# Turning the row maxima of a diffusion transformer's attention with VectorE and DRAM in place of TensorE

## The chip, the cores and the metric

The kernel runs on one core of one Trainium2 chip. The metric is the device time of one execution in microseconds (us); lower is better.

## The reference, cut to what matters

Sixteen images of 256 tokens by 256 features pass through four layers. Layers 0, 2 and 3 are full ones: self attention, cross attention to 120 context tokens, and an MLP of width 1024. Layer 1 has cross attention alone. There are 16 heads of 16 features, all in float32. Of it the change touches only the softmax of the two attentions:

```python
attn = jnp.einsum('bhnd,bhsd->bhns', q, k) * SCALE
attn = jax.nn.softmax(attn, axis=-1)
o = jnp.einsum('bhns,bhsd->bhnd', attn, v)
```

For every query and head the softmax subtracts the largest score of the row before the exponential.

## The kernel before, in words

**Two passes over the scores.** An attention (F is self attention, G cross attention) of one image first makes its scores with the queries in the partitions: steps S0 to S3 for F, S0 and S1 for G (L1287). After each, VectorE takes the maxima over the keys (L978) into `row_max`, 128 queries by 16 heads for each half of the 256 tokens. Then the scores are made again with the keys in the partitions: T0 to T3 for F, T0 and T1 for G (L1309). A last matmul of each T step adds minus the maximum of each query (L1314): it multiplies a one-hot selector `sel` with `max_t`, which must have the heads in the partitions and the 256 queries along the free axis. ScalarE takes the exponential (L1117), and the PV steps (L1340) multiply by the values into `o_acc`; VectorE divides and turns the result in O0 and O1 (L1000 to L1011).

**How the maxima get turned.** Step X (L979 to L992, VectorE) writes minus the maximum in two parts, high and low, for every head into `max_parts`: 128 columns for each half of the tokens, most of them zero. Step M then turns them: TensorE transposes the two 128x128 blocks into a PSUM bank (L1291 to L1295, by way of the helper on L1144), and ScalarE copies the bank to `max_t` (L1103 to L1107). T0 waits for that copy (L1302). There are 48 F jobs and 64 G jobs, so 112 of these turns.

**One score buffer, three ring banks.** S and T steps all use the one four-bank PSUM tensor `score`. TensorE may start the next S or T step only when VectorE's maxima (after an S) or ScalarE's exponential (after a T) have read the one before (L1178 to L1181 and L1193 to L1196). All other matmuls (projections Q, K, V, KV, PR, the MLP's H0 to H3 and F20, F21, the transposes LN and C, and M) go to `ring`, three PSUM banks taken in turn (`RING_STEPS`, L156); a bank is taken again when its reader is done. `o_acc` is one bank, too.

**The order is written out by hand.** Every engine walks the same list of steps and does its own part of each. A word such as `G.T0` names a part (P, F, A for self attention; R, G, B for cross attention; E for the MLP; a leading 1 for layer 1) and a step; `AHEAD` (L145) says which image a part works on in a turn. A word that ends in `.d` marks where VectorE, GpSimd and SyncE do their share of a step, later than TensorE and ScalarE. The first three turns are the list START (L84), the turns 3 to 21 are WITH_L1 (L64), which have layer 1's cross attention in them as well, the turns 22 to 46 are TURN (L49), and the end is TAIL (L116). Since each S or T step has to wait for the reader of the last one, the words on one line of these lists are the work that stands between two score steps.

**SyncE's queue** issues all transfers in the order of the list: q and k are laid out for the scores after the steps Q, K and KV (L646 to L663; four and six transfers), the gates are loaded (`gld`, L716), images are loaded and stored. A wait on SyncE holds up all that stands behind it. `gate_rows` (L284) is a DRAM tensor that the kernel writes and reads again.

Of the kernel before, what the change touches and what calls it, by code (L numbers as in the profile page):

```python
# [13 lines left out]
P = 128  # L14
# [33 lines left out]

TURN = """  # L49
F.S0 f.O1 f.PV3 E.H0  # L50
F.S1 P.V E.RES E.H1 P.V.d
F.S2 P.LN E.H2
F.S3 E.H3 p.N P.gld A.PR F.X A.PR.d
G.S0 F.M B.PR B.PR.d R.C
G.S1 E.F20a E.F20b G.X
F.T0 E.F20b.d R.N P.Q e.N G.M R.A
F.T1 e.A p.A P.Q.d P.K F.PV0
G.T0 c.NC P.RES F.PV1 P.K.d
P.ld R.LN e.LN F.O0 R.RES G.O0
G.T1 E.gld c.AC P.ST R.KV R.KV.d E.F21a G.O1 G.PV0  # L60
F.T2 R.Q G.PV1
F.T3 E.F21b E.F21b.d F.PV2 R.Q.d c.ld
""".split()
# [1336 lines left out]
```

## Time and profile before

| | us |
|---|---|
| median of three runs | 2577.09 |
| lowest, highest | 2574.03, 2577.36 |
| the profiled execution | 2577.71 |
| its span in the profile | 2575.9 |
| TensorE (PE) busy in it | 2479.3 |
| VectorE (DVE) busy | 1858.5 |
| ScalarE (ACT) busy | 1274.0 |
| GpSimd (POOL) busy | 467.2 |

The span is the profiled execution without the 1.8 us around it. Busy time is the union of the instructions of an engine, and ends of matmuls are modelled, so short gaps between matmuls can be hidden in it.

### The profile page before, as it was taken

The page shows a single profiled execution, that of the slowest core. Times are in us where ns is not written, and L with a number is a line of the kernel's source. Part 1 is how long each engine was busy: PE and PEld are TensorE (multiplying, and loading weights), DVE is VectorE, ACT ScalarE, POOL GpSimd, SP SyncE. Part 2 cuts the span into 40 slices and gives each one's busy share as a digit, 9 for nine tenths or more (in the row PEclk, how much of TensorE's full clock was granted, in tenths as well). Part 3 has the DMA queues.
Part 4 walks back from the last instruction along what each step waited for, and adds up shares of the span by engine and source line. Part 5 has one row for each costly group of instructions (what it writes and reads, how often), then busy time and mean ns, then how long its engine had stood idle before and what let it go on. Part 6 is the DMA issues. An engine that isn't in the chain of part 4 may idle for free.

```text
span 2575.9 us, 66165 instructions
## 1 busy us (share of the span) xinstructions
PE 2479.3 (96%) x27466; PEld 1848.3 (72%) x27466; DVE 1858.5 (72%) x3532; ACT 1274.0 (49%) x1810; POOL 467.2 (18%) x510
## 2 busy tenths in 40 slices
PE   5779999999999999999999999999999999999998
PEld 3557777777777777777777777777777777777767
DVE  4767777777777777777777767777677677776752
ACT  1345544555555555555455554554555545445443
POOL 0111211212111211111121211211212212112121
PEclk7889999999999999999999999999999999999999
DMA  5322222222222223232122122132231222222211
GB/s 188 129 93 78 78 74 74 74 80 87 83 77 76 90 81 96 77 101 68 56 76 74 56 76 74 62 96 78 80 107 60 82 84 78 78 66 80 82 33 42
DMA packets 236749, 207.56 MB, mean 81 GB/s; under 512 B 87682, under 2 KB 222020, under 8 KB 236452
## 3 DMA queue, kind: packets, MB, share of 16 engines
q1 hardware_dynamic: 236452, 203.32, 24.7%
q8 instruction: 220, 3.60, 0.6%
q14 instruction: 77, 0.63, 0.1%
HBM read 58.34 MB, written 4.39 MB: 24 GB/s over the span
## 4 chain that ended last, share of the span: by engine, by line
PE 79%; DVE 12%; issue 3%; ACT 3%; SPq 2%; DMA 1%; POOL 1%; DVEq 0%; POOLq 0%; ACTq 0%
PE o_acc L1340 11%; PE score L1287 10%; PE ring L1371 10%; PE ring L1248 10%; PE ring L1362 10%; PE score L1309 8%; PE ring L1352 6%; DVE row_max_F L978 5%; DVE row_max_G L978 5%; PE ring L1144 4%; PE ring L1256 3%; PE score L1314 3%; PE ring L1268 2%; ACT probs L1117 2%; PE ring L1271 2%
## 5 line engine op out<-in xcount | busy, mean ns | idle before, releaser
L1117 ACT ACTIVATE probs<-score 120x2048 f32<-120x2048 f32 (+1 forms) x320 | 601.6, 1880 | 374.8 <-PE score L1314 368.0
L978 DVE TENSOR_REDUCE row_max_F<-score 128x8 f32<-128x2048 f32 x192 | 438.7, 2285 | 103.3 <-PE score L1287 102.8
L1371 PE MATMUL ring<-w_fc,h_t 128*128 128x256 f32 x1536 | 368.9, 386 | 1.0 <-ACT h_t L1128 1.0
L1362 PE MATMUL ring<-x_t_E,w_fc 128*128 128x256 f32 x1536 | 368.3, 386 | 0.0
L978 DVE TENSOR_REDUCE row_max_G<-score 128x16 f32<-128x1920 f32 x128 | 276.1, 2157 | 116.8 <-PE score L1287 116.8
L1128 ACT ACTIVATE h_t<-ring,cols 128x256 f32<-128x256 f32 x384 | 160.7, 470 | 341.1 <-PE ring L1362 341.0
L1362 PEld LDWEIGHTS ring<-x_t_E,w_fc 128*128 128x128 f32 x1536 | 280.8, 190 | 59.3 <-issue 20.3
L1000 DVE STREAM_TRANSPOSE o_turned<-o_acc 128x512 f32<-128x512 f32 x224 | 159.9, 714 | 220.3 <-PE o_acc L1340 220.3
L1371 PEld LDWEIGHTS ring<-w_fc,h_t 128*128 128x128 f32 x1536 | 282.5, 190 | 46.3 <-ACT h_t L1128 1.4
L1340 PE MATMUL o_acc<-probs,v_self 128*17 128x256 f32 x3072 | 204.3, 384 | 0.0
L793 POOL TENSOR_TENSOR x<-x,gated 128x256 f32<-128x256 f32 x96 | 70.3, 733 | 723.1 <-DVE gated L1032 723.1
L1248 PE MATMUL ring<-x_t_P,w_qk 128*128 128x256 f32 x768 | 197.8, 403 | 1.2 <-ACT x_t_P L1068 1.2
L1309 PE MATMUL score<-q_F,k_F 32*128 32x256 f32 x3072 | 166.6, 303 | 8.9 <-ACT probs L1117 5.7
L1309 PEld LDWEIGHTS score<-q_F,k_F 32*128 32x128 f32 x3072 | 119.3, 184 | 75.2 <-issue 55.7
L1248 PEld LDWEIGHTS ring<-x_t_P,w_qk 128*128 128x128 f32 x768 | 143.9, 197 | 35.2 <-issue 8.4
L1287 PEld LDWEIGHTS score<-k_F,q_F 32*128 32x128 f32 x3072 | 106.4, 188 | 84.2 <-DVE row_max_F L978 42.0
L1287 PE MATMUL score<-k_F,q_F 32*128 32x256 f32 x3072 | 146.3, 307 | 21.4 <-DVE row_max_F L978 18.5
L1287 PEld LDWEIGHTS score<-k_G,q_G 32*128 32x128 f32 x4096 | 125.3, 187 | 52.4 <-DVE row_max_G L978 28.0
L1287 PE MATMUL score<-k_G,q_G 32*128 32x120 f32 x4096 | 142.9, 277 | 14.8 <-DVE row_max_G L978 12.0
L787 POOL TENSOR_TENSOR x<-x,gated 128x512 f32<-128x512 f32 x48 | 60.8, 1267 | 423.0 <-DVE gated L1019 423.0
L1340 PE MATMUL o_acc<-probs,v_ctx 120*17 120x256 f32 x2048 | 135.5, 382 | 0.0
L1099 ACT ACTIVATE q_parts<-ring,cols 128x256 fp32r<-128x256 f32 x224 | 94.0, 472 | 80.9 <-PE ring L1248 78.9
(136 smaller groups left out, 3770.9 us busy)
## 6 DMA issues: line engine op xcount, KB each, us to landing
q_G<-q_parts SPq DMA_DIRECT2D x256, 128.0 KB, 2.1
q_F<-q_parts SPq DMA_DIRECT2D x192, 128.0 KB, 2.1
k_F<-k_parts SPq DMA_DIRECT2D x96, 256.0 KB, 2.5
k_F<-k_parts SPq DMA_DIRECT2D x192, 128.0 KB, 2.2
k_G<-k_parts SPq DMA_DIRECT2D x128, 120.0 KB, 2.2
k_G<-k_parts SPq DMA_DIRECT2D x256, 60.0 KB, 1.9
gate_now_P<-gate_rows SPq DMA_DIRECT2D x48, 256.0 KB, 3.2
gate_now_E<-gate_rows SPq DMA_DIRECT2D x48, 256.0 KB, 3.4
```

The source lines that it names most:

```text
L978: nc.vector.tensor_reduce(dst, src, AX.X, ALU.max).then_inc(row_max_ready[r].sem, 1)
L1000: nc.vector.transpose(o_turned[:, :, :, :].rearrange("p i b d -> p (i b d)"), o_acc[:, :])\
L1117: nc.scalar.activation(probs[v % 2][0:keys, :, :], score[0:keys, :].rearrange("p (h q) -> p h q", h=2 * GROUPS), ACT.Exp, scale=SCALE).the ...
L1128: last = nc.scalar.activation(h_t[:, c, :], ps[:, c % 2 * NT:(c % 2 + 1) * NT], ACT.Gelu_apprx_tanh, bias=col(m, "fc1", c))
L1144: return nc.tensor.transpose(dst, src, ident[0:rows_in, 0:rows_in])
L1248: last = mm(ps[:, c * NT:(c + 1) * NT], weight[:, k, at + c * P:at + (c + 1) * P], buffer(x_t, r, m, n)[:, k, :], start=k == 0, stop=k == ...
L1287: last = mm(score[:, col0:col0 + width], q_now[at, c, e, tile * P:(tile + 1) * P].bitcast(F32R), k_now[at, two, c, e, :].bitcast(F32R), st ...
L1309: mm(score[0:keys, g * BANK + e * NT:g * BANK + (e + 1) * NT], k_now[at, two, c, e, tile * P:tile * P + keys].bitcast(F32R), q_now[at, c, ...
L1340: last = mm(o_acc[32 * j:32 * j + HD + 1, i * NT:(i + 1) * NT], v_head, probs[v % 2][0:keys, 2 * j + i, :], start=tile == 0 and (i == 0 or ...
L1352: last = mm(ps[:, t * D:(t + 1) * D], buffer(o_t, r, m, n)[:, k, t * P:(t + 1) * P], weight[:, k, :], start=k == 0, stop=k == KC - 1)
L1362: last = mm(ps[:, c % 2 * NT:(c % 2 + 1) * NT], w_fc1[:, k, c * P:(c + 1) * P], buffer(x_t, r, m, n)[:, k, :], start=k == 0, stop=k == KC - 1)
L1371: last = mm(ps[:, 0:D], h_t[:, k, t * P:(t + 1) * P], w_fc2[:, k, :], start=k == 0, stop=k == MC - 1)
```

## The change

Step M no longer uses TensorE, ScalarE or a ring bank. `max_parts` shrinks to 64 columns (two halves of 32: 16 heads times two parts). VectorE turns it in 32x32 squares at the end of step X. At X SyncE stores the turned squares in a DRAM tensor `max_rows` of 32 rows by 256 queries, which puts the squares side by side. At M SyncE waits for that transfer and loads the 32 rows into `max_t` four times, once for each group of 32 partitions. T0 on TensorE waits for the load. `sel` picks other rows accordingly, and two memsets go. The lists TURN, WITH_L1 and START have a new order throughout, TAIL has the word E14.gld at another place.

```diff
@@ -46,72 +46,73 @@
 
 
 
+
 TURN = """
-F.S0 f.O1 f.PV3 E.H0
-F.S1 P.V E.RES E.H1 P.V.d
-F.S2 P.LN E.H2
-F.S3 E.H3 p.N P.gld A.PR F.X A.PR.d
-G.S0 F.M B.PR B.PR.d R.C
-G.S1 E.F20a E.F20b G.X
-F.T0 E.F20b.d R.N P.Q e.N G.M R.A
-F.T1 e.A p.A P.Q.d P.K F.PV0
-G.T0 c.NC P.RES F.PV1 P.K.d
-P.ld R.LN e.LN F.O0 R.RES G.O0
-G.T1 E.gld c.AC P.ST R.KV R.KV.d E.F21a G.O1 G.PV0
-F.T2 R.Q G.PV1
-F.T3 E.F21b E.F21b.d F.PV2 R.Q.d c.ld
+F.S0 f.PV3 f.O1 E.H0
+F.S1 E.RES P.V E.H1 P.V.d
+F.S2 p.N E.H2 P.LN
+F.S3 E.H3 A.PR F.X A.PR.d
+G.S0 F.M R.C B.PR
+G.S1 B.PR.d E.F20a E.F20b
+F.T0 e.N G.X R.N e.A G.M P.Q R.A P.Q.d
+F.T1
+P.ld F.PV0 E.F20b.d P.K
+G.T0 R.RES c.NC P.K.d F.O0 R.LN e.LN G.O0 F.PV1
+G.T1 R.KV G.PV0 E.F21a E.gld
+F.T2 R.KV.d R.Q G.PV1
+F.T3 G.O1 E.F21b c.AC c.ld p.A P.gld P.RES F.PV2 R.Q.d E.F21b.d P.ST
 """.split()
 WITH_L1 = """
-F.S0 f.PV3 E.H0
-F.S1 1R.C P.V P.V.d P.LN
-F.S2 P.gld E.H1 f.O1 E.H2
-F.S3 F.X 1R.LN E.RES E.H3
-1G.S0 A.PR F.M A.PR.d
-1G.S1 1G.X B.PR E.F20a
-G.S0 E.F20b 1G.M B.PR.d
+F.S0 E.RES 1R.RES f.PV3 E.H0
+F.S1 P.LN P.V P.V.d
+F.S2 E.H1 E.H2 f.O1
+F.S3 1R.LN E.H3
+1G.S0 A.PR B.PR A.PR.d
+1G.S1 P.gld B.PR.d 1R.C E.F20a 1G.X 1G.M
+G.S0 E.F20b F.X R.C E.F20b.d
 G.S1 E.F21a
-1G.T0 1R.RES E.F20b.d P.Q e.N
-1G.T1 R.N e.A P.Q.d 1G.PV0 R.RES G.X 1G.O0 P.K
+1G.T0 e.N P.Q F.M R.N G.X
+1G.T1 P.Q.d 1G.PV0 P.K
 F.T0 E.F21b 1G.PV1
-F.T1 G.M F.PV0 P.K.d R.A
-P.ld 1R.Q E.F21b.d
-G.T0 F.PV1 1G.O1 R.C p.N p.A 1R.KV 1R.Q.d F.O0
-G.T1 G.PV0 1R.KV.d G.O0 R.LN 1B.PR 1p.N 1p.NC
-F.T2 G.PV1 G.O1 R.Q E.gld R.Q.d P.RES
-F.T3 R.KV P.ST 1p.AC 1R.ld 1B.PR.d F.PV2 c.ld 1p.A R.KV.d e.LN
+F.T1 G.M 1p.NC R.A 1R.Q P.K.d 1G.O0 1R.ld E.F21b.d 1G.O1 F.PV0
+G.T0 F.PV1 R.LN 1R.KV e.A 1p.N p.N F.O0 1R.Q.d
+G.T1 R.RES G.PV0 1R.KV.d G.O0 e.LN 1B.PR
+P.ld E.gld 1B.PR.d
+F.T2 P.RES G.O1 G.PV1 R.Q p.A P.ST
+F.T3 R.Q.d 1p.A R.KV R.KV.d c.ld 1p.AC F.PV2
 """.split()
 
 START = """
-W0.v Z0.ZT Z0.ZC P0.N P0.ld P0.A Z0.ZM Z0.ZX W0.cpb W0.proj Z0.ZL P0.LN Z0.ZA W0.raw Z1.ZL P2.ld W0.fc1 P0.Q
-P1.ld W0.self P0.Q.d Z1.ZA P0.K Z0.ZS0 P0.K.d Z1.ZC Z2.ZL Z2.ZA W0.cross P1.N Z0.ZG Z1.ZM Z1.ZX
-F0.S0 P1.A
-F0.S1 P0.V P0.V.d
-F0.S2 P1.LN Z0.ZS1 Z2.ZC
-F0.S3 Z2.ZG Z3.ZL Z2.ZS1 F0.X Z2.ZM Z2.ZX F0.M
-F0.T0 P2.N Z3.ZC R0.ld P1.Q Z3.ZA P1.Q.d F0.PV0
-F0.T1 P1.K Z2.ZS0
-F0.T2 P1.K.d Z3.ZM F0.PV1 P1.V
-F0.T3 P3.ld F0.PV2 F0.O0 Z3.ZG
-F1.S0 W0.fc2 R0.C P1.V.d
-F1.S1 P5.ld P2.A F0.PV3 W0.v2
-F1.S2 F0.O1
-F1.S3 P2.LN P0.RES P0.gld F1.X A0.PR A0.PR.d F1.M
-F1.T0 R0.N Z3.ZX R0.RES P2.Q P2.Q.d R1.ld
-F1.T1 P2.K R0.A P3.N R0.LN P2.K.d F1.PV0 P2.V F1.PV1
-F1.T2 Z3.ZS1 R0.Q P2.V.d
-F1.T3 F1.O0 R0.KV P3.A
-F2.S0 P1.RES W1.l1 F1.PV2 R2.ld R0.KV.d W0.cp
-F2.S1 R0.Q.d
-F2.S2 F1.PV3 F1.O1
-F2.S3 A1.PR F2.X P4.ld
-G0.S0 F2.M
+P0.ld W0.raw P0.N P0.A Z0.ZT Z0.ZC Z0.ZM Z0.ZX Z0.ZL Z0.ZA W0.proj P1.ld Z1.ZL W0.fc1 W0.self P0.LN Z1.ZA P0.Q
+P1.N P0.Q.d Z0.ZG P0.K P0.K.d W0.v Z0.ZS0 Z2.ZA W0.cpb Z2.ZL Z0.ZS1 Z1.ZM Z1.ZC Z1.ZX P1.A
+F0.S0 P0.V P0.V.d P2.ld
+F0.S1
+F0.S2 P1.LN Z2.ZC Z3.ZL W0.cross
+F0.S3 Z2.ZG F0.X F0.M Z2.ZM Z2.ZX P2.N Z3.ZA Z3.ZC
+F0.T0 P1.Q P1.K P1.Q.d P1.K.d F0.PV0 P0.RES Z2.ZS0
+F0.T1
+F0.T2 R0.ld F0.O0 W0.fc2 P0.gld P3.ld F0.PV1 Z3.ZM
+F0.T3 P1.V
+F1.S0 R0.C P2.A F0.PV2 Z2.ZS1 F0.PV3
+F1.S1 F0.O1
+F1.S2 P1.V.d
+F1.S3 F1.X W0.v2 P3.N Z3.ZG P2.LN A0.PR A0.PR.d Z3.ZX P2.Q R0.N F1.M
+F1.T0 R0.A P2.Q.d
+F1.T1 P1.RES R0.RES P2.K
+F1.T2 F1.PV0 P2.V R0.LN R1.ld
+F1.T3 W0.cp P5.ld F1.PV1 P2.K.d P2.V.d R0.Q F1.PV2 F1.O0
+F2.S0 R0.KV R0.KV.d R1.C
+F2.S1 Z3.ZS1 R0.Q.d
+F2.S2 F1.PV3 P4.ld F1.O1
+F2.S3 P1.gld F2.X A1.PR
+G0.S0 F2.M P3.A
 G0.S1 A1.PR.d P3.LN
-F2.T0 G0.X P1.gld R1.C P3.Q G0.M
-F2.T1 P3.K
-G0.T0 R1.N P3.Q.d P3.K.d R1.A F2.PV0 R1.LN F2.PV1 P4.N
-G0.T1 F2.O0 R1.Q G0.O0 G0.PV0
-F2.T2 Z3.ZS0 R1.Q.d G0.O1 P2.RES G0.PV1
-F2.T3 P4.A R1.KV R1.KV.d R1.RES R3.ld P2.gld F2.PV2
+F2.T0 P3.Q G0.X
+F2.T1 G0.M P3.K
+G0.T0 W1.l1 F2.PV0 P4.N P3.Q.d R1.N R1.A P3.K.d P2.gld R1.LN F2.PV1 F2.O0
+G0.T1 G0.O0 R1.Q R2.ld G0.PV0
+F2.T2 G0.PV1 P2.RES P4.A R1.KV R1.Q.d G0.O1
+F2.T3 R1.KV.d R3.ld R1.RES F2.PV2 Z3.ZS0
 """.split()
 TAIL = """
 P15.gld
@@ -134,12 +135,12 @@
 G14.T1 G14.O1 G14.PV0 R15.KV E12.F21a G14.PV1 E13.H0 R15.KV.d E12.F21b E12.F21b.d E13.RES E13.H1 E13.H2
 E13.gld E13.H3
 G15.S0 B14.PR B14.PR.d E14.N
-G15.S1 E13.F20a E13.F20b E14.gld G15.X G15.M
+G15.S1 E13.F20a E13.F20b G15.X G15.M
 G15.T0 E14.LN E14.A
 G15.T1 P12.ST E13.F20b.d G15.PV0 E13.F21a G15.O0 E13.F21b G15.O1 G15.PV1 E14.H0 E14.H2 E14.H1 E14.H3
-E13.F21b.d B15.PR E15.gld E14.F20a B15.PR.d E15.N P13.ST E14.F21a E15.LN E14.F20b E14.RES E15.A E14.F21b
-E15.RES E15.H0 P15.ST E15.H1 E15.H2 E15.H3 E15.F20a E14.F20b.d E15.F21a E15.F20b P14.ST E15.F21b E14.F21b.d
-E15.F20b.d E15.F21b.d
+E13.F21b.d E14.gld B15.PR E15.gld E14.F20a B15.PR.d E15.N P13.ST E14.F21a E15.LN E14.F20b E14.RES E15.A
+E14.F21b E15.RES E15.H0 P15.ST E15.H1 E15.H2 E15.H3 E15.F20a E14.F20b.d E15.F21a E15.F20b P14.ST E15.F21b
+E14.F21b.d E15.F20b.d E15.F21b.d
 """.split()
 
...
-RING_STEPS = ("LN", "C", "Q", "K", "V", "KV", "M", "PR", "H0", "H1", "H2", "H3", "F20a", "F21a",
+RING_STEPS = ("LN", "C", "Q", "K", "V", "KV", "PR", "H0", "H1", "H2", "H3", "F20a", "F21a",
               "ZT", "ZC", "ZM", "ZX", "ZG")
...
+        max_rows = {r: nc.dram_tensor(f"max_rows_{r}", [32, NT], F32, kind="Internal").ap() for r in "FG"}
...
-        max_parts = {r: sb(f"max_parts_{r}", [P, TT, P]) for r in "FG"}
+        max_parts = {r: sb(f"max_parts_{r}", [P, TT, GROUPS, PAIRS, 2]) for r in "FG"}
+        max_turned = {r: sb(f"max_turned_{r}", [P, TT, 32]) for r in "FG"}
...
+                if step == "X":
+                    sp.wait_ge(max_turned_ready[r].sem, max_turned_ready[r].after(m, n))
+                    if max_laid[r].order[m, n] > 0:
+                        sp.wait_ge(max_laid[r].sem(m, n), max_laid[r].after(m, n) - 16)
+
+                    sp.dma_start(max_rows[r].rearrange("h (t a q) -> a h t q", t=TT, a=4), max_turned[r][:, :, :])\
+                        .then_inc(max_written[r].sem(m, n), 16)
+                elif step == "M":
+                    sp.wait_ge(max_written[r].sem(m, n), max_written[r].after(m, n))
+                    t_psum[r].wait_before(sp, m, n)
+                    sp.dma_start(max_t[r][:, :], max_rows[r].unsqueeze(0).to_broadcast([GROUPS, 32, NT]))\
+                        .then_inc(max_laid[r].sem(m, n), 16)
...
-            for r in "FG":
-                nc.gpsimd.memset(max_parts[r][:, :, :], 0.0).then_inc(const_ready, 1)
...
-            nc.vector.tensor_reduce(pair_rows[:, :], ident[:, :].rearrange("p (g w) -> p g w", g=GROUPS)[:, :, 0:8]
-                                    .rearrange("p g (c e) -> p c g e", e=2), AX.XY, ALU.add)\
-                .then_inc(pair_rows_ready, 1)
+            for g in range(GROUPS):
+                at = slice(32 * g, 32 * (g + 1))
+                last = nc.vector.tensor_reduce(pair_rows[at, :], ident[at, 40 * g:40 * g + 2 * PAIRS]
+                                               .rearrange("p (c e) -> p c e", e=2), AX.X, ALU.add)
+            last.then_inc(pair_rows_ready, 1)
...
                     src = row_max[r][:, :, :, :].rearrange("p t g c -> p (t g) c")
-                    parts = max_parts[r][:, :, :].rearrange("p t (g w) -> p (t g) w", g=GROUPS)[:, :, 0:2 * PAIRS]\
-                        .rearrange("p b (c e) -> p b c e", e=2)
-                    if m == 0 and n == 0:
-                        dve.wait_ge(const_ready, CONSTS)
-                    m_psum[r].wait_before(dve, m, n)
+                    parts = max_parts[r][:, :, :, :, :].rearrange("p t g c e -> p (t g) c e")
+                    max_turned_ready[r].wait_before(dve, m, n)
                     dve.wait_ge(row_max_ready[r].sem, row_max_ready[r].after(m, n))
                     nc.vector.tensor_scalar(parts[:, :, :, 0].bitcast(F32R), src, -1.0, None, ALU.mult)\
                         .then_inc(max_hi_ready[r].sem, 1)
@@ -990,6 +1003,12 @@
                     nc.vector.scalar_tensor_tensor(out=parts[:, :, :, 1].bitcast(F32R), in0=src, scalar=-1.0,
                                                    in1=parts[:, :, :, 0], op0=ALU.mult, op1=ALU.subtract)\
                         .then_inc(max_parts_ready[r].sem, 1)
+                    dve.wait_ge(max_parts_ready[r].sem, max_parts_ready[r].after(m, n))
+                    if max_written[r].order[m, n] > 0:
+                        dve.wait_ge(max_written[r].sem(m, n), max_written[r].after(m, n) - 16)
+                    nc.vector.transpose(max_turned[r][:, :, :].rearrange("p t h -> p (t h)"),
+                                        max_parts[r][:, :, :, :, :].rearrange("p t g c e -> p (t g c e)"))\
+                        .then_inc(max_turned_ready[r].sem, 1)
...
-                elif step == "M":
-                    act.wait_ge(m_psum[r].sem, m_psum[r].after(m, n))
-                    t_psum[r].wait_before(act, m, n)
-                    nc.scalar.activation(max_t[r][:, :].bitcast(F32R), ps[:, 0:NT], ACT.Identity)\
-                        .then_inc(max_t_ready[r].sem, 1)
...
-                elif step == "M":
-                    pe.wait_ge(max_t_ready[r].sem, max_t_ready[r].after(m, n))
...
-                elif step == "M":
-                    pe.wait_ge(max_parts_ready[r].sem, max_parts_ready[r].after(m, n))
-                    for t in range(TT):
-                        last = transpose(ps[:, t * P:(t + 1) * P], max_parts[r][:, t, :], P)
-                    last.then_inc(m_psum[r].sem, 1)
...
-                        pe.wait_ge(max_t_ready[r].sem, max_t_ready[r].after(m, n))
+                        pe.wait_ge(max_laid[r].sem(m, n), max_laid[r].after(m, n))
```

The rest of the diff declares or drops the semaphores that these lines use (`max_turned_ready`, `max_written` and `max_laid` come, `m_psum` and `max_t_ready` go).

## Rows read from the trace of the kernel before

**Rows 1.** the page: busy shares of the engines, and the chain that ended last, by engine

```profile
...
PE 2479.3 (96%) x27466; PEld 1848.3 (72%) x27466; DVE 1858.5 (72%) x3532; ACT 1274.0 (49%) x1810; POOL 467.2 (18%) x510
...
PE 79%; DVE 12%; issue 3%; ACT 3%; SPq 2%; DMA 1%; POOL 1%; DVEq 0%; POOLq 0%; ACTq 0%
...
```

**Rows 2.** busy us by stage: PE, PEld, DVE, ACT, POOL; then PEclk, DMA share, GB/s

```profile
...
0.00:150.80 150.80, 104.67 (x1086) 71.21 (x1086) 88.26 (x184) 44.82 (x58) 12.74 (x26) 0.83 0.45 150
...
300.00:1265.60 965.60, 949.54 (x11015) 703.79 (x11014) 743.70 (x1424) 501.33 (x712) 174.87 (x187) 1.00 0.25 80
1265.60:2432.20 1166.60, 1161.78 (x12751) 873.27 (x12750) 849.27 (x1587) 601.63 (x853) 223.28 (x238) 1.00 0.24 76
2432.20:2575.90 143.70, 128.95 (x1128) 100.19 (x1124) 68.49 (x128) 58.27 (x91) 25.07 (x28) 0.98 0.14 45
...
```

**Rows 3.** groups by line and shape: count | busy us, mean ns | idle before

```profile
...
L978 DVE TENSOR_REDUCE row_max_F<-score 128x8 f32<-128x2048 f32 x192 | 438.7, 2285 | 103.3 <-PE score L1287 102.8
...
L1000 DVE STREAM_TRANSPOSE o_turned<-o_acc 128x512 f32<-128x512 f32 x224 | 159.9, 714 | 220.3 <-PE o_acc L1340 220.3
...
L1011 DVE STREAM_TRANSPOSE o_t_B<-o_norm 128x256 f32<-128x256 f32 x128 | 57.0, 445 | 4.4
...
L1144 PE MATMUL ring<-ident,max_parts_G 128*128 128x128 f32 x128 | 25.6, 281 | 0.0
...
L1144 PE MATMUL ring<-ident,max_parts_F 128*128 128x128 f32 x96 | 20.3, 294 | 0.8 <-DVE max_parts_F L990 0.8
...
```

**Rows 4.** TensorE in one turn with layer 1: start us, us

```profile
...
740.33 0.38 PE L1144 MATMUL ring<-ident,max_parts_F 128*128 128x128 f32 x2
740.90 1.11 PE L1287 MATMUL score<-k_G,q_G 32*128 32x120 f32 x32 [0.19 <-DVE row_max_G L978]
...
743.77 1.89 PE L1371 MATMUL ring<-w_fc,h_t 128*128 128x256 f32 x8
745.59 1.11 PE L1287 MATMUL score<-k_G,q_G 32*128 32x120 f32 x32
...
749.04 1.11 PE L1287 MATMUL score<-k_G,q_G 32*128 32x120 f32 x32 [0.20 <-DVE row_max_G L978]
...
752.41 0.50 PE L1309 MATMUL score<-q_G,k_G 32*120 32x256 f32 x8 [0.34 <-DVE row_max_G L978]
...
```

**Rows 5.** TensorE in one turn without layer 1: start us, us

```profile
...
2029.42 0.44 PE L1144 MATMUL ring<-ident,max_parts_F 128*128 128x128 f32 x2
2029.69 1.89 PE L1352 MATMUL ring<-w_cp,o_t_B 128*128 128x256 f32 x8
2031.42 0.37 PE L1144 MATMUL ring<-ident,x_hat_C 120*128 120x120 f32 x2
2031.82 1.11 PE L1287 MATMUL score<-k_G,q_G 32*128 32x120 f32 x32
...
2039.25 0.38 PE L1144 MATMUL ring<-ident,max_parts_G 128*128 128x128 f32 x2
2039.56 0.51 PE L1309 MATMUL score<-q_F,k_F 32*128 32x256 f32 x8
...
```

**Rows 6.** DMA issues: KB each, us to landing

```profile
...
gate_now_E<-gate_rows SPq DMA_DIRECT2D x48, 256.0 KB, 3.4
...
context<-in_ctx_dram SPq DMA_DIRECT2D x32, 120.0 KB, 2.3
...
gate_rows<-h_t SPq DMA_DIRECT2D x6, 32.0 KB, 2.1
...
```

**Rows 7.** all engines near the end: VectorE's X, then TensorE's T0

```profile
...
2495.67 0.19 DVE L990 SCALAR_TENSOR_TENSOR max_parts_G<-row_max_G,max_parts_G 128x32 fp32r<-128x32 f32 x1
...
2496.98 0.51 PE L1309 MATMUL score<-q_G,k_G 32*120 32x256 f32 x8 [0.57 <-ACT max_t_G L1106]
...
```

**Rows 8.** TensorE in turn 3: start us, us

```profile
...
160.82 1.23 PE L1287 MATMUL score<-k_F,q_F 32*128 32x256 f32 x16 [2.87 <-DVE row_max_F L978]
162.76 3.75 PE L1352 MATMUL ring<-w_proj,o_t_A 128*128 128x256 f32 x8 [0.71 <-DVE o_t_A L1011]
...
```

More of the change, by code:

```diff
@@ L382, in build_program @@
         s_psum = signals("s_psum", "FG", {"F": 4, "G": 2})
-        m_psum = signals("m_psum", "FG")
         t_psum = signals("t_psum", "FG", {"F": 4, "G": 2})
@@ L394, in build_program @@
         k_high_ready = signals("k_high_ready", "FG")
-        max_t_ready = signals("max_t_ready", "FG")
         probs_ready = signals("probs_ready", "FG", {"F": 4, "G": 2})
@@ L409, in build_program @@
         max_parts_ready = signals("max_parts_ready", "FG")
+        max_turned_ready = signals("max_turned_ready", "FG")
         o_turned_ready = signals("o_turned_ready", "FG", 2)
@@ L429, in build_program @@
         k_laid = semaphore("k_laid")
+        max_written = {r: Turns([semaphore(f"max_written_{r}")], self_order if r == "F" else cross_order) for r in "FG"}
+        max_laid = {r: Turns([semaphore(f"max_laid_{r}")], self_order if r == "F" else cross_order) for r in "FG"}
         x_stored = semaphore("x_stored")
@@ L473, in build_program @@
         projects = {"F": "A", "G": "B"}
-        CONSTS = 8
+        CONSTS = 6
         q_jobs = [(attends[r], m, n) for r, m, step, n, here in steps if step == "Q"]
```

## The prediction

> **What bounds the kernel now.** I read the page's busy shares and its chain first: TensorE is busy 96% of the span and holds 79% of the chain, VectorE holds 12% [rows 1]. Then the stages. The turns 6 to 21 (with layer 1) take 965.6 us, 60.4 each; the turns 22 to 46 take 1166.6, 46.7 each. TensorE stands idle for only 16 us of the first and 5 us of the second; head and tail lose 46 and 15 us [rows 2]. By these shares any work taken from TensorE should come off the time. The timeline of single turns says otherwise, and that decides my forecast: `score` is one buffer, so between two S or T steps there is a least distance. After a G S step of 1.04 us the next score step begins 3.4 us after the start of the last (745.59 to 749.04, and 749.04 to 752.41), each time with an idle of 0.2 to 0.3 us released by VectorE's maxima [rows 4]; the maxima themselves take 2.29 us for F [rows 3] and a little less for G. Where the ring work in such a slot is shorter than about 2.4 us, it is free, and taking it away gives a wait.
>
> **What step M costs.** TensorE is busy 25.6 + 20.3 = 45.9 us with the 224 transposes [rows 3], 0.41 us for each of 112 jobs; from start to start a pair takes 0.27 or 0.31 us [rows 5], about 33 us in all. Those are the upper ends of what can be won.
>
> Where do they stand? **Turns with layer 1** have three. The ones after 1G.S0 and before G.S1 stand in slots that VectorE ends: M at 740.33 is over at 740.6, and the next S starts at 740.90 on the maxima [rows 4]. They win nothing where they are. In the new list their places are taken: 1G.S0's slot gets both PR steps (3.65 us, no wait), 1G.S1's and G.S0's slots get a C transpose beside F20a or F20b : 0.27 to 0.40 [rows 5] and 1.82 from 743.77 to 745.59 [rows 4] are 2.1 to 2.2, again under 2.4. The three slots were 3.44 + 4.69 + 3.45 = 11.58 us and become 4.69 + 3.44 + 3.44, and 0.15 more, since VectorE does B.PR.d and X with its new turn before G.S0's maxima: 11.72, so +0.14. The two C steps left other slots: -0.53, but F.S1's slot then holds only LN and V (2.4) and waits 0.12. F.T1's slot loses an M and is long enough (1R.Q and a PV remain, 2.9): -0.36. Sum -0.63, say -0.6 for each turn, **-10 us** for 16 turns.
>
> **Turns without layer 1.** G.S0's slot holds M, PR and C: 0.27 + 1.73 + 0.40 = 2.40, exactly the least distance [rows 5]. The new list keeps C and PR there: 2.13 of work and 0.27 of wait, nothing won. F.T0's slot holds Q and M, 2039.56 being the next T; the exponential would let T1 start 0.1 earlier, and without M it does. The other slots keep their work. -0.1 for each turn, **-2.5 us** for 25. So some 14 us of M's time in these turns becomes wait.
>
> **What is added on VectorE.** A transpose of 64 columns. The two in the trace take 714 ns for 512 and 445 for 256 columns [rows 3], 1.05 ns a column, hence 0.24 us; ends are 0.19 (the smallest operation beside it [rows 7]) and 0.445. 112 x 0.24 = 27 us on an engine busy 72% [rows 1]; its only exposed part is the 0.15 above. The four small reductions that make `sel`, the two memsets less and the 112 ScalarE copies less all lie beside longer waits: nothing.
>
> **What is added as latency.** The store: 32 KB to DRAM; the nearest row lands in 2.1 us, the other end is the 3.4 of a 256 KB broadcast from DRAM. The load: 128 KB in 1 KB rows; the nearest is the context load, 120 KB in the same shape, 2.3 us, and I add 0.2 for reading each row four times; the same 3.4 is its upper end and 2.1 the lower for both [rows 6]. With SyncE's own 0.1 that is 4.8 us from the end of X's turn to T0 (4.3 to 6.9). On SyncE's queue the M of an image waits about 2 us for its store; behind it stand P.Q's and P.K's layouts, which have most of a turn until the next F.S0, so I give nothing for that. P.gld now stands ahead of 1G.X, but what it waits for is done in the slot before.
>
> Is the latency covered? The tightest places: 1G.X ends 4.7 us after the start of 1G.S1 (step 1.15, maxima 2.2, B.PR.d 0.68, X 0.7), 1G.T0 is due at 10.3 (three S slots): 5.6 us against 4.8. G.X in a turn without layer 1 ends 4.85 after G.S1's end, G.T0 is due at 10.4: 5.6 against 4.8. Both are covered with 0.8 to spare; the F jobs have over 3 us.
>
> Here the Trainium skill speaks against the change: DMA: Bandwidth & Descriptors, Specifications, says that transfers with pieces below 512 B are written by read-modify-write, and the store consists of 128-byte pieces. No row here shows such a store to DRAM; it enters the sum with nothing, and its sign is that of the second rival.
>
> **The tail** keeps its order but for a gate load, and there nothing covers the latency. In G14, X ends at 2495.86 and T0 starts at 2496.98 [rows 7]; now it would be 2495.9 + 0.25 + 4.8 = 2500.9, 3.9 later. G15 has the same pattern, 3.9 again. Some 2 us of the first are taken up by waits for x_hat that follow it anyway; F15.M's own place saves 1; I add 2 for a lower granted clock after these gaps (the head, full of gaps, has a mean of 0.83 against 1.00 in the turns [rows 2]). **+7 us**.
>
> **The head.** TensorE idles for 46 of 150.8 us [rows 2]. The new list asks for x, w_raw and the conditioning vector earlier and lets P0.K's layout no longer wait behind Z0's gates and loads: some 3.5 us earlier F0.S0. Against this F0.M's and F1.M's latency is exposed (about +3 and +1), and denser T slots give 2 or 3 back: -2. In turn 3 PR waits 0.71 for o_t after an S step that had itself waited 2.87, and then runs at half pace, 3.75 against 1.89 for the same step in rows 5 [rows 8]; the new list moves O1 a slot forward and puts both PR steps behind S3: -4 with the filled slot before. Turns 4 and 5: -1. **-7 us**, and this is the least certain term (-17 to +6).
>
> **Sum.** -10 - 2.5 + 7 - 7 = -12.5. The profiled execution took 2577.71 (span 2575.9 and 1.8 around it), 0.6 above the median of 2577.09. From the median: 2564.6, rounded 2565.
>
> **The rivals.**
> First, all of TensorE's M time comes off: for it speaks the 99.6% busy share in the turns 22 to 46, against it the slots of rows 4 and 5. It gives 2577 - 46 + 7 = 2538, or 2551 with the 33 us of pitch. Chance 0.13.
> Second, the way through DRAM lands late, at 1G.T0 and G.T0 of each turn. With both transfers at 3.4 us the latency is 6.9, 2.1 more than I take; 0.8 is spare, so 1.3 us is lost in 16 + 25 turns, 53 us: 2618. It decides from 1.1 us above my value (0.8 and 12.5/41 = 0.3): 5.9 us. Against it: the 2.1 and 2.3 of rows 6 are medians under the same traffic. With the excess halfway it is 2590. Chance 0.14. The skill's rule on small pieces would bring this one about.
> Third, the orders win nothing: head and tail cost more than I think (gaps lower the clock), and the turns' -12 is used up: 2577, within 0.2%. Chance 0.13.
> My forecast: 0.60, with its own range 2552 to 2572.
>
> **Range and chances.** 2546 to 2588 takes in most of the first rival by pitch, the third, and the mild part of the second. A measurement of this kernel can tell about 0.2%, 5 us, from no change. Faster by more: 0.60 + 0.13 = 0.73, less 0.02 for the top of my own range, 0.71. Within it: 0.14. Slower: 0.15.
>
> **What would show it.** Right: M's transposes and the copies are gone; the turns with layer 1 last about 59.8 us and those without 46.6; TensorE's busy time falls by some 40 us and its idle time rises by some 30, with "VectorE's maxima" as releaser of the score steps. 1G.T0 and G.T0 start on the exponential or the maxima, not on the load of `max_t`; in G14 and G15 T0 does wait for that load, 4 us. The store lands in about 2.1 us, the load in 2.5; VectorE's turn is 0.24. Wrong: T0 waiting for the load in every turn (second rival), or TensorE's idle time unchanged (first), or F3.S0 later than 150.9 us.

## The result, and the profile after

| | before | after |
|---|---|---|
| median of four runs each, us | 2575.56 | 2649.62 |
| lowest, highest | 2573.84, 2577.36 | 2640.79, 2653.45 |
| span of the profiled execution | 2575.9 | 2647.8 |

The ratio is 1.0283 (95% interval 1.0255 to 1.031): the change makes the kernel 74 us slower. I had forecast 2565, and the range ended at 2588.

The first lines to read are the page's busy shares and its chain, which answer to [rows 1]:

```profile
PE 2473.2 (93%) x27242; PEld 1827.6 (69%) x27242; DVE 1850.2 (70%) x3647; ACT 1236.5 (47%) x1698; POOL 467.1 (18%) x508
...
PE 66%; DVE 13%; DMA 12%; issue 6%; ACT 2%; SPq 1%; POOL 0%; DVEq 0%; POOLq 0%; ACTq 0%
```

The 224 transposes and 112 copies are gone. TensorE's busy time falls by only 6 us, though, where I had 40. DMA held 1% of the chain and now holds 12%, TensorE's share falls from 79% to 66%. The waits of TensorE (us in total, times, longest) say on what:

```profile
PE score L1316 <- DMA max_t_G<-max_rows_G: 72.5, 47, 6.8
...
PE score L1316 <- DMA max_t_F<-max_rows_F: 4.6, 4, 1.9
```

T0 of cross attention waits for the load of `max_t` 47 times. Which of its two transfers is late? The timeline of one turn without layer 1, all engines, start and us:

```profile
2083.57 0.24 DVE L1009 STREAM_TRANSPOSE max_turned_G<-max_parts_G 128x64 f32<-128x64 f32 x1
...
2083.84 0.52 SPq L681 DMA_DIRECT2D max_rows_G<-max_turned_G  x1
...
2086.17 0.52 SPq L686 DMA_DIRECT2D max_t_G<-max_rows_G  x1
...
2091.26 0.51 PE L1316 MATMUL score<-q_G,k_G 32*120 32x256 f32 x8 [1.70 <-DMA max_t_G<-max_rows_G]
```

VectorE's turn takes the 0.24 us of the forecast. SyncE waits for the store before it issues the load, so the store has landed 2.33 us after its issue. The load then takes 5.09 us until T0 starts, where I had 2.5. In a turn with layer 1, TensorE:

```profile
775.08 0.50 PE L1316 MATMUL score<-q_G,k_G 32*120 32x256 f32 x8 [1.87 <-DMA max_t_G<-max_rows_G]
...
775.98 3.41 PE L1260 MATMUL ring<-x_t_P,w_qk 128*128 128x256 f32 x8
```

The load was issued at 770.57, 4.51 us before. Behind the wait the projection Q takes 3.41 us, where [rows 5] have 1.89 for a step of as many matmuls; the clock granted in these 3.41 us is 0.56 of full, and in T0 just ahead of them still 1.00. The tail shows it most, TensorE again:

```profile
2559.96 0.79 PE L1316 MATMUL score<-q_G,k_G 32*120 32x256 f32 x8 [6.58 <-DMA max_t_G<-max_rows_G]
...
2564.22 3.75 PE L1260 MATMUL ring<-x_t_R,w_q 128*128 128x256 f32 x8 [0.72 <-ACT x_t_R L1087]
```

There the granted clock is 0.50, the lower of the two levels (1.2 for 2.4 GHz). But the kernel before had short waits at this place too, and its Q already took 3.15 us:

```profile
2501.15 3.15 PE L1248 MATMUL ring<-x_t_R,w_q 128*128 128x256 f32 x8
```

By stage, the columns as in [rows 2]; the bounds are the starts of F.S0 in turns 3, 6, 22 and 47:

```profile
0.00:163.10 163.10, 108.73 (x1082) 71.91 (x1082) 88.80 (x193) 43.49 (x54) 14.70 (x26) 0.80 0.45 143
163.10:318.20 155.10, 135.38 (x1484) 99.98 (x1484) 106.20 (x216) 67.79 (x94) 27.05 (x29) 0.94 0.28 86
318.20:1294.40 976.20, 936.65 (x10926) 692.74 (x10922) 744.25 (x1472) 485.07 (x665) 179.93 (x188) 1.00 0.29 87
1294.40:2490.10 1195.70, 1159.80 (x12658) 860.27 (x12654) 841.92 (x1639) 583.50 (x801) 218.81 (x236) 1.00 0.26 81
2490.10:2647.80 157.70, 132.66 (x1116) 102.73 (x1116) 69.04 (x131) 56.68 (x87) 26.66 (x29) 0.93 0.16 47
```

All stages are longer: 12.3 us to turn 3, 5.9 in turns 3 to 5, 10.6 in turns 6 to 21, 29.1 in turns 22 to 46 and 14.0 in the tail, whose granted clock is 0.93 for 0.98 before.

### The profile page after: what moved, and what is told of

It reads as the page before. It is cut to its first block, busy times and chain, and to the rows that moved or that the text cites. A ratio compares the mean times of both kernels' runs of the same rounds, so it can differ in the third digit from the quotient of the medians.

```text
span 2647.8 us, 66048 instructions
## 1 busy us (share of the span) xinstructions
PE 2473.2 (93%) x27242; PEld 1827.6 (69%) x27242; DVE 1850.2 (70%) x3647; ACT 1236.5 (47%) x1698; POOL 467.1 (18%) x508
## 4 chain that ended last, share of the span: by engine, by line
PE 66%; DVE 13%; DMA 12%; issue 6%; ACT 2%; SPq 1%; POOL 0%; DVEq 0%; POOLq 0%; ACTq 0%
PE ring L1369 11%; PE o_acc L1347 10%; PE score L1299 9%; DMA max_t_G<-max_rows_G 8%; PE score L1316 7%; PE ring L1260 7%; PE ring L1359 6%; PE ring L1378 5%; DVE row_max_F L994 5%; DMA max_rows_G<-max_turned_G 4%; DVE row_max_G L994 3%; PE ring L1280 2%; PE score L1321 2%; PE ring L1158 2%; PE ring L1283 2%
## 5 line engine op out<-in xcount | busy, mean ns | idle before, releaser
L797 POOL TENSOR_TENSOR x<-x,gate_now_P 128x512 f32<-128x512 f32 x48 | 64.1, 1336 | 720.7 <-DMA gate_now_P<-gate_rows 694.6
L1316 PE MATMUL score<-q_G,k_G 32*120 32x256 f32 x2048 | 112.3, 305 | 77.8 <-DMA max_t_G<-max_rows_G 72.5
L1316 PEld LDWEIGHTS score<-q_G,k_G 32*120 32x120 f32 x2048 | 81.4, 181 | 128.7 <-issue 98.8
L865 DVE SCALAR_TENSOR_TENSOR k_parts<-ring,cols,k_parts 128x256 fp32r<-128x256 f32 (+1 forms) x224 | 78.9, 394 | 120.9 <-ACT k_parts L1118 120.8
```

The costliest lines, as they stand in the source:

```text
L865: last = nc.vector.scalar_tensor_tensor(out=parts[:, 1, c, 0:width].bitcast(F32R), in0=src[:, c * width:(c + 1) * width], scalar=row_col(m ...
L1316: mm(score[0:keys, g * BANK + e * NT:g * BANK + (e + 1) * NT], k_now[at, two, c, e, tile * P:tile * P + keys].bitcast(F32R), q_now[at, c, ...
```

## The experiments

Theory A: the load repeats its 32 rows in the outermost dimension of the transfer, of size four, and so is spread over four DMA engines at most. Its rivals: it is its size, the fourfold reading of the same rows, the queue in front of it, or DRAM itself (theory B in the texts below); or the load is not the matter, and the new orders cost the time (theory C).

**The load split in four.** Same bytes, same rows, no repeat inside a transfer:

```diff
-sp.dma_start(max_t[r][:, :], max_rows[r].unsqueeze(0).to_broadcast([GROUPS, 32, NT]))
+for g in range(GROUPS):
+    sp.dma_start(max_t[r][32 * g:32 * (g + 1), :], max_rows[r])
```

> The changed kernel, with the load of max_t as four transfers of 32 rows, one for each group of 32 partitions, in place of one whose outermost dimension repeats four times. Same bytes, same order, same rows of DRAM. Theory A (the repeat over four as the outermost dimension lets the load run on few DMA engines, so that it takes 4.5 to 5 us where 2.5 was assumed): the last of the four lands about 3.5 us after the first issue, T0 of G waits over 1 us less in each turn and in the tail, time about 2618 us. Theory B (reading back what was just stored in DRAM, or the store of 128-byte pieces, is slow by itself): as long as the changed kernel or longer by the three more issues, 2650 us. Theory C (the new order costs the time, whatever the way): no gain, 2650 us.

It took 2592.71 us, ratio 1.0069 (1.0054 to 1.0084), so 57 of the 74 us are gone, and the time is 25 below what I expected of theory A. Issues of the load (KB each, us to landing), then TensorE's wait for it:

```profile
max_t_G<-max_rows_G SPq DMA_DIRECT2D x256, 32.0 KB, 1.8
```

```profile
PE score L1317 <- DMA max_t_G<-max_rows_G: 23.3, 16, 5.6
```

The rows are still read four times, at 1.8 us a piece. That speaks for A, and leaves "128 KB in one transfer" as a rival. Of the 23.3 us that remain, 11.2 stand in the tail; each load now takes four issues on SyncE, 1.7 us for the four.

**The order alone**, the maxima turned by TensorE as before (F.M in the turns with layer 1 stands four words earlier, since a ring bank has to be free):

```diff
-TURN, WITH_L1, START, TAIL of before
+TURN, WITH_L1, START, TAIL of after
```

> The kernel before with the new lists TURN, WITH_L1, START and TAIL (step M of F stands ahead of F21a in the turns with layer 1, so that F21a keeps its ring bank). TensorE still turns the maxima. Theories A and B (the way through DRAM costs the time): within 10 us of the kernel before, 2567 to 2587 us, turns without layer 1 at 46.7 us and with it at 60 to 61. Theory C: well over, 2600 us or more.

2607.46 us, ratio 1.0124 (1.0109 to 1.0139), a miss of 20 us at least. It even lies beyond the 2600 that I had set as the mark of theory C, so this run by itself speaks for the order as the cause; what speaks against it are the runs below that have the same new order and a prompt load, or no wait. The turns 6 to 21 take 982.5 us (before 965.6) and the turns 22 to 46 1177.2 (1166.6). Its waits on TensorE:

```profile
PE ring L1144 <- DVE max_parts_G L990: 19.1, 16, 1.3
...
PE ring L1248 <- DVE gated L1032: 6.8, 25, 0.3
```

In the new list 1G.M stands right behind 1G.X. SyncE can wait there at no cost to TensorE; TensorE's own transposes can't, and cost 1.2 us in each of 16 turns, more than the 16.9 lost there. The order is made for the new way and is bad for the old one. So it doesn't split off as a cost of its own.

**The way alone**, in the order of before (the new tail, and P.gld of image 1 ahead of 0's X of cross attention):

```diff
-TURN, WITH_L1, START of after
+TURN, WITH_L1, START of before
```

> The changed kernel with the old order of TURN, WITH_L1 and START (P1.gld stands ahead of G0.X in START, the tail is the changed one, since SyncE's queue would lock up otherwise). In the old order X of 1G and of G come right behind the maxima, about 0.7 to 1.8 us earlier against the T0 that needs them. Theories A and B: the way costs some 7.3 us from the turn to T0 in either order; the wait at G.T0 of the turns without layer 1 falls from 1.7 us to about 0.3, that of 1G.T0 from 1.9 to under 0.5, the tail stays 14 us longer than before; 2590 us. Theory C: the time is that of the kernel before or better, 2575 us, with the tail's waits.

2675.78 us, ratio 1.0393 (1.0377 to 1.0409), 86 above what was expected. Waits of TensorE:

```profile
PE score L1316 <- DMA max_t_G<-max_rows_G: 74.2, 36, 6.7
...
PE score L1316 <- DMA max_t_F<-max_rows_F: 20.0, 23, 6.9
```

SyncE's issues in one turn with layer 1 show a second cost that I hadn't seen:

```profile
792.66 0.56 SPq L686 DMA_DIRECT2D max_t_F<-max_rows_F  x1
793.32 0.52 SPq L681 DMA_DIRECT2D max_rows_G<-max_turned_G  x1
797.64 0.53 SPq L686 DMA_DIRECT2D max_t_G<-max_rows_G  x1
...
811.45 0.56 SPq L681 DMA_DIRECT2D max_rows_G<-max_turned_G  x1
813.80 0.56 SPq L686 DMA_DIRECT2D max_t_G<-max_rows_G  x1
```

Right behind F's slow load, the store of 1G takes 4.32 us until its load can be issued; with nothing ahead of it the next takes 2.35. The busy share of the DMA engines shows why (columns as in [rows 2]):

```profile
795.40:796.40 1.00, 0.85 (x4) 0.39 (x3) 1.00 (x1) 0.00 (x0) 0.00 (x0) 1.00 0.27 95
796.40:797.00 0.60, 0.34 (x12) 0.34 (x16) 0.60 (x2) 0.00 (x0) 0.00 (x0) 1.00 0.33 54
```

The load's bytes run until 796.4, and only then do those of the store, issued at 793.32; they are known by their pace, 54 GB/s for 0.6 us, where a store alone in the tail of the changed kernel has 52. There they start 1.2 us after the issue, here 3.1. So the store's bytes come behind the load's. The old order has F's M and 1G's X side by side, the new one keeps them apart. Alone the order costs 32 us and the way 100; together they cost 74. That the new order hides a part of the latency and keeps stores from behind loads fits this.

**No wait.** T0 reads a constant, the steps, transfers and orders are the changed kernel's:

```diff
-pe.wait_ge(max_laid[r].sem(m, n), max_laid[r].after(m, n))
...
-                                      max_t[r][at, :].bitcast(F32R),
+                                      max_none[at, :].bitcast(F32R),
```

> The changed kernel, in which the last matmul of a T step reads a constant tile of zeros in place of max_t, so that T0 does not wait for the load; store, load and VectorE's turn still run. The maximum is left out of the softmax, and the scale of the exponential is a hundredth, so that it stays finite; durations do not depend on either. Theories A and B: all that the way costs beyond my forecast is the wait of T0 (77 us of TensorE idle before the first score matmul of a T step and lower clock behind it): 2560 to 2570 us. Theory C: 2620 us or more.

2564.01 us, ratio 0.9955 (0.9939 to 0.9972). By stage:

```profile
297.40:1253.60 956.20, 935.36 (x10922) 691.35 (x10918) 745.29 (x1471) 485.01 (x665) 180.00 (x188) 1.00 0.30 89
1253.60:2420.30 1166.70, 1158.16 (x12654) 859.39 (x12650) 845.46 (x1639) 583.76 (x801) 218.90 (x236) 1.00 0.27 83
```

All transfers still run, and the turns are as long as before or shorter, so the traffic and SyncE's queue cost nothing that shows there: the wait is worth 2647.8 - 2562.2 = 85.6 us of span, 20.8 of it up to turn 6, 20.0 and 29.0 in the two kinds of turns, 15.8 in the tail. Theory C has fallen with this run.

**32 rows in one load.** Only the rows that the selector needs, to every fourth partition, by way of DRAM:

```diff
-sp.dma_start(max_t[r][:, :], max_rows[r].unsqueeze(0).to_broadcast([GROUPS, 32, NT]))
+sp.dma_start(max_t[r][0:P:4, :], max_rows[r])
```

> The changed kernel with the store to DRAM as it is, and the load cut to one transfer of 32 rows that puts head row h into partition 4h, so that each group of 32 partitions gets the eight rows it needs and 96 partitions of max_t stay zero; sel picks every fourth row. 32 KB in place of 128, one issue, 32 as the outermost dimension. Theory A (few engines on the repeated load): it lands in about 1.9 us, near a single one of the four loads (1.7 to 1.8), 1 us before the last of four; turns at 59.8 and 46.7 us, tail 153, time about 2585 us, 8 below the four loads. A rival, D: the DRAM tensor just written is slow to read whatever the shape: the load takes 3 us or more, time 2592 us or more.

2577.45 us, ratio 1.0008 (0.9998 to 1.0017), 8 us below what I expected; rival D, slow DRAM, has fallen. The load lands in 2.1 us, the turns 22 to 46 take 1166.6, and in the tail T0 waits 4.72 and 4.50.

**No DRAM.** Four transfers of 8 KB at M take the squares from SBUF to SBUF, in the new and in the old order:

```diff
-sp.dma_start(max_rows[r]..., max_turned[r][:, :, :])
-sp.dma_start(max_t[r][:, :], max_rows[r].unsqueeze(0).to_broadcast([GROUPS, 32, NT]))
+for i in range(4):
+    sp.dma_start(max_t[r][0:P:4, :].rearrange("h (t a q) -> h t a q", t=TT, a=4)[:, :, i, :],
+                 max_turned[r][32 * i:32 * (i + 1), :, :])
```

> As before this one, but without DRAM: at step M four transfers bring the turned squares straight from VectorE's tile to max_t, one for each block of 32 queries, 32 partitions to every fourth partition, 8 KB each. One landing in place of two on the way. Theory A, with two hops as the rest of the loss: the last lands 1.8 + 2.0 = 3.8 us after the first issue, about 3.5 us sooner than in the changed kernel; no wait at T0 in the turns (59.8 and 46.7 us each), the tail at 149, the head at 153: 2572 to 2576 us, no different from the kernel before. D: about 2580.

> The same straight way with the old order of the kernel before (tail and one gate load as in the run with the way alone). If the new order is what makes M's place worth something, this gives turns with layer 1 of 60 us or more (two of three M places are slots that the maxima end) and 46.6 without it, 2578 to 2584 us with the tail's waits. If the order is worth nothing, the same as with the new order.

The new order took 2579.12 us, ratio 1.0015 (1.0006 to 1.0024), the old one 2590.16, 1.0054 (1.0037 to 1.0071), 3 and 6 us above the ranges that I had expected. Without DRAM nothing is won over the load of 32 rows: once the load is prompt, the way through DRAM is covered in the turns. The pair also gives the worth of the new order for a prompt load, 11 us. By stage it is no even gain. The turns 22 to 46 in the old order, columns as in [rows 2]:

```profile
1274.70:2438.10 1163.40, 1153.61 (x12655) 861.86 (x12654) 859.41 (x1637) 584.87 (x803) 223.40 (x238) 1.00 0.26 78
```

These are 3.2 us shorter than before, and with the new order (1166.6) they are not; the turns 6 to 21 take 961.1 in the old order and 957.9 in the new one, and most of the new order's gain in the two profiled executions, 8 us of 8.4, lies ahead of turn 6.

**Two loads that repeat twice each**, the sharpest form of theory A:

```diff
+for half in range(2):
+    sp.dma_start(max_t[r][64 * half:64 * (half + 1), :], max_rows[r].unsqueeze(0).to_broadcast([2, 32, NT]))
```

> The changed kernel with two loads, each repeating the 32 rows twice, in place of one that repeats them four times. Same bytes. Theory A in its sharpest form (as many DMA engines as the outermost dimension counts, here two for each load): no better than the one load, though each is half as large: T0's waits as in the changed kernel or longer, 2650 us or more. If instead the size or the repeat as such costs the time, each of the two lands sooner than the one: 2620 us or less.

2782.24 us in two executions, ratio 1.0804 (1.0773 to 1.0835). Its waits, and a turn from its timeline:

```profile
PE score L1317 <- DMA max_t_G<-max_rows_G: 134.0, 49, 8.0
```

```profile
2090.93 1.04 SPq L687 DMA_DIRECT2D max_t_G<-max_rows_G  x2
...
2097.04 0.51 PE L1317 MATMUL score<-q_G,k_G 32*120 32x256 f32 x8 [2.37 <-DMA max_t_G<-max_rows_G]
```

Two transfers of half the size take 6.1 us where one takes 5.1. The size of a single transfer as the cause has fallen; what fits is the smaller outermost dimension, with both loads on the same engines.

**The repeat inside.** One load of 128 KB, each row read four times, as in the changed kernel; only the repeat is the second dimension. This one tells A from the size and the fourfold reading:

```diff
-sp.dma_start(max_t[r][:, :], max_rows[r].unsqueeze(0).to_broadcast([GROUPS, 32, NT]))
+sp.dma_start(max_t[r][:, :], max_rows[r].unsqueeze(1).to_broadcast([32, 4, NT]))
```

> One load of 128 KB again, with the same 32 rows of max_rows each read four times, but the repeat is the second dimension of the source instead of the first: partition 4h+i gets row h (the selector picks partition 4h, as in the kernel with the load of 32 rows). Bytes, rows, order and steps are the changed kernel's. Theory A, the outermost dimension of a transfer sets over how many DMA engines it is spread (4 in the changed kernel, 32 here): the load lands in 2.1 to 2.6 us, T0 in the turns no longer waits for it beyond 10 to 25 us in all, and the time is within 0.3% of the load of 32 rows, 2577 to 2585. Rival B, what takes the time is the size of 128 KB or that each row is read four times: the load lands in 5 us, as in the changed kernel, and the time stays at 2645 to 2655.

2579.09 us, ratio 1.0009 (1.0 to 1.0018). The load, and TensorE's waits for it in the whole span:

```profile
max_t_G<-max_rows_G SPq DMA_DIRECT2D x64, 128.0 KB, 2.4
```

```profile
PE score L1314 <- DMA max_t_G<-max_rows_G: 10.6, 4, 4.9
```

2.4 us instead of 4.5 to 5.1, with the same bytes from the same rows in one transfer. The time lost to that one dimension is 2647.8 - 2577.4 = 70.4 us of span.

How many engines carry the load can be read from the DMA share where nothing else is under way, since it is the mean busy share of 16. Ahead of T0 of G14 in the tail, the changed kernel, the two loads, and the repeat inside:

```profile
2557.90:2559.20 1.30, 0.00 (x0) 0.00 (x0) 0.07 (x1) 0.00 (x0) 0.00 (x0) 0.60 0.27 95
...
2692.00:2695.20 3.20, 0.00 (x0) 0.00 (x0) 0.82 (x1) 0.00 (x0) 0.67 (x1) 0.50 0.12 39
...
2490.40:2490.60 0.20, 0.00 (x0) 0.00 (x0) 0.20 (x1) 0.00 (x0) 0.20 (x1) 1.00 0.87 307
```

A share of 0.27 is about four engines of 16, 0.12 about two, and 0.87 nearly all; 95, 39 and 307 GB/s go with them. Two loads of a repeat of two never pass 0.15 in this stretch, so both are on the same two engines. (The share can read too high, 1.09 in one stretch of the last run, so the counts are rough.) Theory A stands. It does not explain all of the time: T0 there starts 4.24 us after the issue, and 2.51 with the repeat inside. Of these 1.7 us the flow of the bytes takes 0.6 (1.3 us against 0.7). They also begin 0.8 us later (2.2 us after the issue against 1.3), and T0 follows their end 0.3 later. Why isn't shown, only that it goes with the same dimension.

**The ends reordered.** With a prompt load the tail and the head still cost more than before. Eight lines of the lists are changed, here two of the tail's (F21a and F21b come ahead of T0, and G14.M goes up):

```diff
-G14.S1 G14.X E12.F20a R15.N E12.F20b E12.F20b.d G14.M R15.RES
+G14.S1 G14.X G14.M E12.F20a R15.N E12.F20b E12.F20b.d E12.F21a E12.F21b E12.F21b.d R15.RES
-G15.S1 E13.F20a E13.F20b G15.X G15.M
+G15.S1 E13.F20a E13.F20b G15.X G15.M E13.F21a E13.F21b
```

> The kernel whose single load reads the 32 rows that matter (its shifts and its order otherwise the changed kernel's), with eight places of the written order changed at the two ends: in turns 14 and 15 of layer 2 the pieces F21a and F21b stand between X and T0, where TensorE otherwise waits 4.5 to 4.7 us for the load, P1.Q goes ahead of F0.T0, F0.X ahead of Z2.ZG, and F2.PV0 ahead of G0.T0. My theory: the long turns are as in the kernel before (46.66), the turns with layer 1 0.8 us better each, and all that keeps the time at 2577 is the tail (153.5 us, before 143.7) and the head (158.3, before 150.9). Then the waits ahead of the last two T0 fall under 1 us, Q behind them runs at full pace, the tail falls to 142 to 145 and the head to about 154, and the time is 2566 (2561 to 2570), 0.4% under before. Rival: the tail is bound by the chain of the last experts, which the pieces only shift; then it stays at 150 to 153 and the time at 2574 to 2577.

> The same places of the written order changed at the two ends, in the kernel whose four transfers go from SBUF to SBUF with no DRAM between. My theory: tail 151.8 to 142 to 145, head 155.1 to about 152, time 2567 (2562 to 2571). Rival as in the run beside it: the tail stays at 150 and the time at 2575 to 2579.

With the load of 32 rows 2569.74 us, ratio 0.9968 (0.9956 to 0.9981): this version is 0.3% faster than the kernel before. With the direct transfers 2571.06, 0.9978 (0.9968 to 0.9989). TensorE at T0 of G14 and G15 in the first:

```profile
2488.43 0.51 PE L1317 MATMUL score<-q_G,k_G 32*120 32x256 f32 x8 [1.04 <-DMA max_t_G<-max_rows_G]
...
2520.44 0.50 PE L1317 MATMUL score<-q_G,k_G 32*120 32x256 f32 x8 [1.02 <-DMA max_t_G<-max_rows_G]
```

The waits fall from 4.7 and 4.5 to 1.0, and the tail from 153.5 to 146.8. That is 2 us short of what I expected, and 3 above the tail of before. The same moves were not tried in the kernel before, so how much of the 0.3% the new way needs isn't known.

## Why the prediction was wrong

Lengths against the span of before, in us:

| stage | before | forecast | after | no wait | repeat inside | best version |
|---|---|---|---|---|---|---|
| to turn 6 | 300.0 | -7 | +18.2 | -2.6 | +1.6 | +0.4 |
| turns 6 to 21 | 965.6 | -10 | +10.6 | -9.4 | -10.6 | -11.4 |
| turns 22 to 46 | 1166.6 | -2.5 | +29.1 | +0.1 | +0.6 | +0.1 |
| tail | 143.7 | +7 | +14.0 | -1.8 | +9.9 | +3.1 |
| sum | 2575.9 | -12.5 | +71.9 | -13.7 | +1.5 | -7.8 |

**The step that failed: "The load: 128 KB in 1 KB rows; the nearest is the context load, 120 KB in the same shape, 2.3 us, and I add 0.2 for reading each row four times".** The shape was not the same: the context's outermost dimension is 120 rows, the load's is the repeat of four. It took 4.5 to 5.1 us, outside even my upper end of 3.4 [rows 6]. With the repeat inside it takes 2.4, so the number was right for the transfer that I had in mind. The Trainium skill has the rule, in DMA: Bandwidth & Descriptors, Rules for kernel authors, on the use of all 16 engines: an outermost dimension below 16, such as a leading repeat, keeps the transfer to at most that many engines. The changed kernel and both runs with another repeat agree with it (4.5 to 5.1 us and a DMA share of 0.27 at four, 6.1 and 0.12 at two and two, 2.4 and 0.87 at 32 rows). The same page says under "Why a DMA increments its semaphore by 16 and not by 1" that such a transfer takes the lowest-numbered engines, which would put two small ones on the same pair. The 0.12 agrees that they share one; which pair it is no row names. I had picked the rule on small pieces from that page, and that one did not bite: the store of 128-byte pieces landed in 2.3 us, against 2.1 for the row that I took. The store's DRAM side has an outermost dimension of four as well; with a quarter of the bytes that cost no more than these 0.2 us.

The latency was also added up wrongly, 2.1 + 2.5 + 0.1 being 4.7 and not 4.8, which changes nothing.

**That the latency would be covered was right for a prompt load.** I gave 0.8 us to spare at a latency of 4.8. With the repeat inside, T0 of the turns waits for the load 0.2 us in all between 300 and 2423 us. The changed kernel's latency in the turn shown is 2091.26 - 2083.81 = 7.45, and the second rival, whose rule starts at 5.6, gives 41 x 1.85 = 76 us and 2641. It was the right rival, with a chance of 0.14, but the reason that I gave it (the store) was wrong, and its upper end too low. That its 2641 comes so near is partly luck: the wait costs 49 us in these turns and not 76, and 37 at the two ends, for which the rival had nothing.

**The turns with layer 1** came out close, once the load is prompt: -10 forecast, -9.4 and -10.6 in the table, -12.9 with 32 rows and -7.7 without DRAM. The slots behind the -10 were not checked one by one, so how near it is may be luck. **The turns without** win nothing, where I had 2.5. The 2.5 is there in the old order (-3.2 without DRAM), and the new order gives it back; at which step isn't shown. The slots are bound by the reader of `score`, as read from [rows 4, 5], and the first rival has fallen: in the run without a wait TensorE does 50 jobs of M less in turns 22 to 46 and these take 1166.7 us. One mark that I set was wrong, though: busy time there fell only from 1161.8 to 1158.2, not by M's time of some 20 us. The ends of matmuls are modelled, so that short waits can count as busy, which fits. The 99.6% [rows 2] was no statement that TensorE bounds the stage.

**The head** is the second miss: -7 forecast, +1.6 with a prompt load. The 4 us for turn 3 didn't come. TensorE there after the change, to be laid beside [rows 8]:

```profile
173.05 1.23 PE L1299 MATMUL score<-k_F,q_F 32*128 32x256 f32 x16 [2.88 <-DVE row_max_F L994]
174.99 3.75 PE L1359 MATMUL ring<-w_proj,o_t_A 128*128 128x256 f32 x8 [0.71 <-DVE o_t_A L1030]
```

Wait and half pace are what they were. F0.S0 did come earlier, by 3.4 us as forecast (32.8 for 36.2), and what followed ate it: F3.S0 starts at 163.1, and with the repeat inside at 154.9, in both later than the 150.9 that I had named as a sign of being wrong.

**The tail** costs 9.9 us at the latency that I assumed, not 7: the two waits, 4.9 with the repeat inside and 4.7 and 4.5 with 32 rows, are near the 4.5 that follows from my 3.9 and the 0.57 of [rows 7]. So the rest was wrong, the 3 us that I took off or the 2 that I added for the lower clock; the runs don't part them. At the changed kernel's latency the tail costs 14.0.

Of the 84 us between forecast and span, 70 are the load, 9 the head, 3 the tail and 3 the turns without layer 1; those with it give back 1. Even with a prompt load I would have been wrong on the sign: at 1.0009 the third rival, orders that win nothing at the ends, would have been the outcome.

**Left open.** The head was not taken apart word by word; which of its new places gives back the 3.4 us isn't shown. Nor is the cost of the lower clock behind long waits shown by itself: no run kept TensorE busy with idle work there. Nor is the later start of the bytes in the load with the repeat outside.

## What to carry to other kernels

When a transfer repeats data, look at which dimension is outermost: rows outside and the repeat inside, or no repeat at all with a selector that takes other rows. To price a transfer by a row of the trace, compare its outermost dimension too, not bytes and row length alone. And where every step on the critical path alternates between two engines, work taken off one of them becomes wait: take the price of a removed step from the distance between the starts of the steps around it, and fill the ends, where nothing covers a new latency, with work moved from behind it.

## What the runs showed of the hardware that I had not expected

- One dimension of a transfer doubles its time: 128 KB in 1 KB rows from DRAM took 4.5 to 5.1 us (4.2 in the tail) with the repeat of four outermost, and 2.4 with 32 rows outermost. Two such loads of 64 KB with a repeat of two took 6.1 in the turn shown.
- The DMA share counts the engines of a transfer that runs alone: 0.27 with four outermost, 0.12 with two loads of two, 0.87 with 32.
- A store of 32 KB to DRAM in 128-byte pieces landed in 2.3 us, and the load of 32 KB behind it in 2.1.
- After a wait of 6.58 us in the tail the projection Q ran for 3.75 us at a granted clock of 0.50 (3.15 before the change, 1.99 in a turn before), and after one of 1.87 with layer 1 for 3.41 at 0.56. In the turns this added little: against the run without a wait they lose (1195.7 - 1166.7) / 25 = 1.16 us each, and (976.2 - 956.2) / 16 = 1.25 with layer 1, beside waits of 27.5 / 25 = 1.10 and 24.2 / 16 = 1.51.
- A store issued 0.66 us behind a load on a quarter of the engines took 4.32 us to land instead of 2.35; its bytes began when the load's had ended.
